# A two-layer attention and feed-forward block on one core: the last batches' hand-over, and the first turn's input split, put in another order

## The reference

```python
qkv = relu(einsum('bnc,oc->bno', x, qkv_weight))           # q, k, v: 32 heads of 8
vk = einsum('bnhe,bnhd->bhed', concat([v, 1]), k)
vk_q = einsum('bhed,bnhd->bnhe', vk, q)
y = (vk_q[..., :8] / (vk_q[..., 8:] + 1e-15)) @ proj_weight.T + proj_bias
x = layernorm(x + y)
h = silu(x @ w_gate.T / 127) * (x @ w_up.T / 127)          # integer weights, 768 hidden units
x = layernorm(x + h @ w_down.T / 127)
```

## Time and profile before

| | |
|---|---|
| median of 3 runs | 500.27 us (499.93 to 500.87) |
| the profiled execution | 500.56 us, its span 498.5 us |
| PE busy | 487.9 us of the span, 98% |
| DVE busy | 418.3 us, 84% |
| ACT busy | 231.8 us, 46% |
| POOL busy | 88.1 us, 18% |
| DMA | 66.42 MB, mean 133 GB/s |

### The profile page before, as it was taken

How to read it: one execution, slowest core, us unless ns; L and a number is a source line. 1 busy time by engine, 2 the same in 40 slices (tenths; PEclk the granted TensorE clock), 3 DMA queues, 4 the chain that set the end, 5 groups by cost and what they waited for, 6 DMA issues and landing times.

```text
span 498.5 us, 11660 instructions
## 1 busy us (share of the span) xinstructions
PE 487.9 (98%) x4580; PEld 423.3 (85%) x4580; DVE 418.3 (84%) x963; ACT 231.8 (46%) x393; POOL 88.1 (18%) x70
## 2 busy tenths in 40 slices
PE   9999999999999999999999999999999999999886
PEld 5888888888889888898888889888888888888775
DVE  5776978888888897988888888897988888798966
ACT  4666435453453625435452453625435452364453
POOL 1320111311121131111311111131111212014012
PEclk9999999999999999999999999999999999999999
DMA  8323162361714527062351705427062441631212
GB/s 313 152 86 128 44 196 102 108 232 42 232 62 172 165 84 252 2 232 103 132 205 49 250 38 179 158 84 252 19 227 90 151 145 62 210 112 43 87 43 85
DMA packets 49512, 66.42 MB, mean 133 GB/s; under 512 B 3024, under 2 KB 33488, under 8 KB 49488
## 3 DMA queue, kind: packets, MB, share of 16 engines
q1 hardware_dynamic: 49344, 65.82, 38.1%
q10 hardware_dynamic: 144, 0.26, 0.1%
HBM read 35.66 MB, written 23.59 MB: 119 GB/s over the span
## 4 chain that ended last, share of the span: by engine, by line
PE 81%; DVE 8%; issue 4%; DMA 3%; ACT 2%; POOL 1%; SPq 0%; POOLq 0%; DVEq 0%
PE up_ps L991 29%; PE abcd_ps L991 23%; PE gate_ps L991 22%; PE abcd_ps L1043 3%; DVE h L570 2%; PE gate_ps L1021 2%; DVE st L639 1%; DVE h_lo L563 1%; DMA att_way<-wg_raw 1%; PE gate_ps L1162 1%; POOL rstd L298 1%; ACT h_hi L375 1%; DMA wkv_raw<-att_way 1%; DMA wd_raw<-x_way 1%; ACT silu L380 1%
## 5 line engine op out<-in xcount | busy, mean ns | idle before, releaser
L298 POOL TENSOR_TENSOR rstd<-ve,minus_half 128x4 f32<-128x4 f32 (+2 forms) x36 | 43.9, 1219 | 323.6 <-DVE ve L651 323.5
L570 DVE SCALAR_TENSOR_TENSOR h<-up_ps,silu 128x512 f32<-128x512 f32 x95 | 65.4, 688 | 29.6 <-PE up_ps L991 16.2
L375 ACT ACTIVATE h_hi<-h 128x512 fp32r<-128x512 f32 (+1 forms) x97 | 60.6, 625 | 54.9 <-DVE h L570 54.3
L380 ACT ACTIVATE silu<-gate_ps 128x512 f32<-128x512 f32 x95 | 55.7, 587 | 54.6 <-PE gate_ps L991 54.6
L991 PE MATMUL up_ps<-x1T_hi,wu_hi 128*128 128x512 f32 x192 | 75.0, 390 | 1.4 <-DVE h L570 1.4
L991 PE MATMUL gate_ps<-x1T_hi,wg_hi 128*128 128x512 f32 x192 | 74.9, 390 | 0.4 <-ACT silu L380 0.4
L991 PE MATMUL gate_ps<-x1T_lo,wg_hi 128*128 128x512 f32 x192 | 75.0, 391 | 0.0
L991 PE MATMUL up_ps<-x1T_lo,wu_hi 128*128 128x512 f32 x192 | 74.7, 389 | 0.0
L563 DVE TENSOR_TENSOR h_lo<-h,h_hi 128x512 fp32r<-128x512 f32 (+1 forms) x97 | 64.2, 677 | 0.5 <-ACT h_hi L375 0.2
L372 ACT ACTIVATE kv<-abcd_ps 128x512 f32<-128x512 f32 x55 | 32.9, 601 | 65.1 <-PE abcd_ps L991 65.1
L321 POOL TENSOR_TENSOR xb<-x_raw,bias_sb 128x1024 f32<-128x1024 f32 x16 | 38.7, 2421 | 73.2 <-DVE den L593 71.0
(11 more groups left out here) (181 smaller groups left out, 1064.2 us busy)
## 6 DMA issues: line engine op xcount, KB each, us to landing
x_raw<-x_tok SPq DMA_DIRECT2D x16, 512.0 KB, 5.5
att_way<-wg_raw SPq DMA_DIRECT2D x30, 256.0 KB, 2.9
wkv_raw<-att_way SPq DMA_DIRECT2D x30, 256.0 KB, 3.0
out<-out_sb SPq DMA_DIRECT2D x15, 512.0 KB, 2.7
xT_raw<-x_chan SPq DMA_DIRECT2D x14, 512.0 KB, 5.9
x_way<-wu_raw SPq DMA_DIRECT2D x28, 256.0 KB, 2.1
wd_raw<-x_way SPq DMA_DIRECT2D x28, 256.0 KB, 3.0
x<-r SPq DMA_DIRECT2D x13, 512.0 KB, 4.0
```

The source lines that it names most:

```text
L298: nc.gpsimd.tensor_tensor(rs[:, tiles], ve[:, tiles], minus_half[:, tiles], ALU.pow).then_inc(rs_ok, 1)
L375: nc.scalar.activation(dst, src, ACT.Copy).then_inc(ok, 1)
L380: nc.scalar.activation(silu[:, j % 2, :], gate_ps[bank_of(j)][:], ACT.Silu, scale=WSCALE).then_inc(silu_ok[j], 1)
L570: nc.vector.scalar_tensor_tensor(out=h[:, j, :], in0=up_ps[bank_of(j)][:], scalar=WSCALE, in1=silu[:, j % 2, :], op0=ALU.mult, op1=ALU.mul ...
```

## The change

It has four parts. PE begins down of batch 14 when its first `h_lo` blocks and `r1_ok[0]` are there, with tiles 0, 1 and 2 side by side, and tile 3 alone behind them. Batch 13 is normed into `att` in place of `out_sb` and stored from there, under a semaphore of its own, so that DVE norms batch 14 into `out_sb` without waiting for that store. In the first turn ACT and DVE split batch 3's input sooner. In turn 14 ACT splits `attT` one block later, and DVE does the statistics of batch 13's second norm ahead of its share of that split.

```diff
@@ SP
-            store(NB - 3)
-            store(NB - 2)
+            sp.wait_ge(out_in_att_ok, 1)
+            sp.wait_ge(stored, 16 * (NB - 3))
+            sp.dma_start(out[NB - 3], att[:].rearrange("p t c -> p (t c)")).then_inc(stored, 16)
+            sp.wait_ge(out_ok, NB - 2)
+            sp.dma_start(out[NB - 2], out_sb[:].rearrange("p t c -> p (t c)")).then_inc(stored, 16)
@@ ACT, ffn_step (turn 1 alone)
                     silu_of(i - 1, j)
+                    if j == 0 and isinstance(i, int) and i == 1:
+                        xT_hi_of(3)
                     if j < NH - 3:
                         h_hi_of(i - 1, j)
-                    if j == 1 and isinstance(i, int) and i == 1:
-                        xT_hi_of(3)
@@ ACT, step_before_last (turn 14)
-                    if j == 0:
+                    if j == 1:
                         attT_hi_spread(i)
@@ ACT, during gate_up(15)
-            act.wait_ge(stored, 16 * (NB - 3))
-            out_tiles(2, out_sb, r2_own, rstd1, range(2))
+            out_tiles(2, att, r2_own, rstd1, range(2))
...
-                    last = out_tiles(2, out_sb, r2_own, rstd1, (2 + j,))
+                    last = out_tiles(2, att, r2_own, rstd1, (2 + j,))
                     if j:
-                        last.then_inc(out_ok, 1)
+                        last.then_inc(out_in_att_ok, 1)
@@ DVE, first_turn
-                h_of(0, 0, 1)
+                h_of(0, 0)
+                xT_lo_of(3)
+                h_of(0, 1)
                 h_lo_of(0, 0)
...
                 h_of(0, 3)
-                xT_lo_of(3)
                 attT_lo_spread(1)
@@ DVE, turn 14
             h_of(i - 1, 0)
+            stats_2(i - 1)
+            h_of(i - 1, 1)
+            variance_2(i - 2)
             attT_lo_spread(i)
-            h_of(i - 1, 1)
-            stats_2(i - 1)
             h_of(i - 1, 2)
             att_blocks(i + 1)
             h_of(i - 1, 3)
-            variance_2(i - 2)
@@ DVE, during gate_up(15)
-            dve.wait_ge(out_ok, i - 2)
-            out_of(i - 2)
+            dve.wait_ge(stored, 16 * (i - 3))
+            dve.wait_ge(rstd2_ok, i - 1)
+            normed(out_sb, r2, mv2, rstd2, out_ok)
@@ DVE, ahead of the sums of batch 15, which overwrite r2_own
+            dve.wait_ge(out_in_att_ok, 1)
@@ PE, down of batch 14
-            pe.wait_ge(h_ok[NH - 1], i)
+            pe.wait_ge(r1_ok[0], i + 1)
             for blocks in (range(4), (4,), (5,)):
-                for t in range(2):
+                for t in range(3):
                     last = down_part(i - 1, t, blocks, last_down[t])
-            last.then_inc(down_mm[0], 1)
-            for t in (2, 3):
-                pe.wait_ge(r1_ok[t - 2], i + 1)
-                last = down_part(i - 1, t, range(NH), last_down[t])
-            last.then_inc(down_mm[1], 1)
+                    if NH - 1 in blocks and t == 1:
+                        last.then_inc(down_mm[0], 1)
+            pe.wait_ge(r1_ok[1], i + 1)
+            down_part(i - 1, 3, range(NH), last_down[3]).then_inc(down_mm[1], 1)
```

More of the change, by code:

```diff
@@ L163, in build @@
         rstd1_pair, x1_pair = signals("rstd1_pair", 2), signals("x1_pair", 2)
-        neg_mean2_ok, shift2_ok, out_last_ok = signal("neg_mean2_ok"), signal("shift2_ok"), signal("out_last_ok")
+        neg_mean2_ok, shift2_ok, out_last_ok, out_in_att_ok = (
+            signal(f"{n}_ok") for n in ("neg_mean2", "shift2", "out_last", "out_in_att"))
         down_tile, r2_tile, st2_tile, out_tile = (signal(f"{n}_tile") for n in ("down", "r2", "st2", "out"))
```

## The result

| | before | after |
|---|---|---|
| median of the runs | 500.57 us (4 runs, 499.93 to 500.98) | 493.74 us (4 runs, 493.46 to 493.91) |
| profiled execution | 500.56, span 498.5 | 493.46, span 491.5 |
| ratio of the times | | 0.9862, interval 0.9848 to 0.9876 |

What follows compares the result with a forecast made beforehand. The prediction took PE, busy 487.9 of 498.5 us at full clock, as the bound, gaining only where it waits. Terms 0.97 + 2.0 + 1.38 + 1.75 + 0.45 = 6.55 us off 500.27 gave 493.7 us, range 492.8 to 496.2.

Steps and rivals of the forecast that it cites:

- (a): First turn: with the earlier split, PE's stall before proj_of(1) and the restart go whole, 0.97 us.
- (3): First turn: batch 4's earlier load delays the attT reads, so proj_of(1) stays late; 494.7 us, chance 0.10.
- (b): Turn 14: new order on ACT and DVE shortens PE's 25.36 us stretch by 2.0 us, lower bound 0.8.
- (c): Down of batch 14: early start with three tiles side by side takes 6.35 us instead of 7.73, gaining 1.38.
- (d): gate_up(15): the norm no longer waits for batch 13's store, so 10.91 us instead of 12.66, gaining 1.75.
- (e): Down of batch 15: 6.29 us against a clean 5.76; gain 0.45, with 0.08 left for PSUM hand-over.
- It fits, by 0.1 us: Down of 15: block 5's h_lo is ready at 486.69, PE gets there at 486.81.
- The 6.16 us: Down of 15: time from DVE's norm start to PE's last 28 matmuls before, used to place block 5's h_lo.
- (2): Last 20 us: DVE becomes the bound, PE waits 1.4 us in gate_up(15) and down of 15; 495.1 us, chance 0.17.
- (4): Whole kernel: only the idle time in PE's records is won, 4.3 us; 496.0 us, chance 0.05.
- (5): Whole kernel: the change doesn't do what it says, waits stay; within 0.2% (1.0 us), chance 0.02.
- (6): First turn: early load slows the attT reads so far that the kernel is slower; 501.3 us and more, chance 0.02.

Runs made afterwards that it cites:

- no_first: The changed kernel with the first turn's split of batch 3's input put back in its old place: 494.89 us, ratio to before 0.9892.
- two_tiles: The changed kernel with down of batch 14 begun early but tiles 0 and 1 side by side, then 2, then 3: 494.33 us, ratio to before 0.9875.
- old_down: The changed kernel with down of batch 14 as before, waiting first for the last h, two tiles together: 495.23 us, ratio to before 0.9901.
- dve14_old: The changed kernel with DVE's order in turn 14 as before and ACT's as changed: 495.38 us, ratio to before 0.9898.
- by_two_again: Repeat of the changed kernel with down of 14's first four blocks taken two and two over three tiles: 493.37 us, ratio to before 0.9854.
- act14_old: The changed kernel with ACT's order in turn 14 as before and DVE's as changed: 495.20 us, ratio to before 0.9895.
- old_store: The changed kernel with batch 13 normed into and stored from out_sb again: 495.77 us, ratio to before 0.9916.
- dve_plus_one: The changed kernel with one unused 512-column DVE operation added behind the norm of batch 14: 493.98 us, ratio to before 0.9868.
- old_turn14: The changed kernel with both ACT's and DVE's order in turn 14 as before: 495.70 us, ratio to before 0.9906.

## Why the prediction was right, point by point

**(a) The first turn** gave 0.97, as predicted. Its rival (3) had the earlier load right: that of batch 4's input is now issued at 44.97 us instead of 51.71. The two reads of `attT` are no longer alike as in the earlier trace rows; the tile's view of the kernel after:

```profile
DMA to landing us min/median/max: 2.7/3.3/3.9
```

The first takes 2.7 us, the second 3.9 where it took 3.0. In the twelve other traces the slower read takes 3.1 us in no_first, which has the late load, and 2.9 to 4.5 in the eleven with the early one: 3.6 or more in seven, 3.2 or less in four (two_tiles, old_down, dve14_old, by_two_again). So with the early load the slower read took up to 1.5 us more than the 3.0 of the earlier trace rows, and in four traces next to nothing more; what decides it is open. It doesn't reach `attT_hi`, which starts at 48.47 without a wait for it and has none in any of these traces, though in act14_old the read (44.3 + 4.5 = 48.8) is only just there for the second half of it (48.82). The case needed a landing after 51.5; here it is 44.5 + 3.9 = 48.4.

**(b) Turn 14** gave 1.98 for 2.0. The step that mattered was the choice between what PE's records show as idle (0.8) and the idle time of DVE's first half (2.0). The experiments bear out the second: each engine's old order alone makes DVE idle 1.7 to 1.9 us, and the stretch is longer by as much. In one point the prediction said too little: it spoke of the order on both engines as one term, and did not see that half of it would be worth 0.03 or 0.27 us.

**(c) Down of 14** gave 1.39 for 1.38. The working put PE's restarts 0.60 and 1.20 us after the end of `gate_up(14)`; they came at 464.42 - 463.81 = 0.61 and 465.02 - 463.81 = 1.21. That the third tile covers the wait for block 5 is shown by two_tiles, though its worth of 0.69 us is not only the data's lateness. No wait for block 4 is seen there with two tiles either. The new wait `r2_ok[1]` cost nothing: `gate_up(15)` is 10.91 us long, which is clean.

**(d) `gate_up(15)`** gave 1.75 for 1.75, and old_store took exactly this back.

**(e) Down of 15** gave 0.54 for 0.45. No run shows the 0.08 us held back for a hand-over of PSUM: 5.63 + 0.12 = 5.75 us, 48 matmuls at the clean pitch. Mis-sized was the step "It fits, by 0.1 us": the spare is 0.55 us at block 5, and the nearest point is block 4, which the step did not look at, with 0.36. The 6.16 us were not DVE's time but PE's. They end where PE began block 5 (490.37), and PE came there late by its own stalls, the doubt that the second case named. DVE's timeline has the block itself, in two halves, before and after:

```profile
489.60 0.76 DVE L563 TENSOR_TENSOR h_lo<-h,h_hi 128x256 fp32r<-128x256 f32 x2 [0.15 <-ACT h_hi L375]
...
482.48 0.76 DVE L566 TENSOR_TENSOR h_lo<-h,h_hi 128x256 fp32r<-128x256 f32 x2 [0.16 <-ACT h_hi L379]
```

Both begin 5.39 us after the norm (484.21 and 477.09), and the first half is there some 0.42 later, after 5.81. That is 0.35 less than 6.16. Another 0.09 us is the norm, which began 6.94 us after `gate_up(15)` (477.09 - 470.15) and not 7.03. The term came out, since the step found it to fit all the same.

**The other cases.** (2), DVE as the bound in the last 20 us, did not come, but dve_plus_one shows how near it is: one more operation of 0.60 us is enough. The DVE starts of the earlier trace rows, less than their durations apart, were the right measure; the end did not lose the 1.4 us of that case. The prediction set against them the Trainium skill ("VectorE: DVE Perf Modes", The DRAIN you can't avoid), by which the next operation doesn't start until the pipeline is empty. The same paragraph adds that an operation that isn't held starts earlier, and these rows agree with that (0.68 us of duration, 0.60 from start to start), so the disagreement that the prediction saw is only with the first half of the rule. (4), idle time in the records only, fell with old_turn14. (5) and (6) fell with the table of stretches. The sum was 6.55 and the five stretches gave 6.63. Undone one at a time, the four parts cost 0.98, 1.75, 1.41 and 2.28 us, 6.42 in all, so they add up, and none covers for another. The medians differ by 6.83; the 0.2 that is left is less than the start of the head varies from one execution to the next, and no run settles it. That the time came out at 493.74 for 493.7 is in part luck: the gain was 0.28 us more than the sum, and the median before, with its fourth run, 0.30 more than the 500.27 that the forecast started from.

## What to carry to other kernels

Where one engine is never idle for long, measure a stretch by the starts at its ends against its clean length, not by the idle time that is shown: in turn 14 that was 2.0 us against 0.8. Look then for the engine whose idle time has the same size; an order has to be mended on every engine that hands work to it, since either half alone gave 0.03 or 0.27 us of 1.98. Before an early start is called free, walk the consumer through every block it asks for, with the end of the producer's own row for each, and not with the time at which the consumer took it before.

## What the runs showed of the hardware

- A wait of PE ends 0.05 to 0.06 us after DVE's operation at a plain matmul (465.29 to 465.35, 482.64 to 482.69), and 0.30 us after it where PE stood at a compare-and-branch (467.36 to 467.66), whose own record takes 0.20 of it. The branch as cause was only argued.
- After a wait the first matmul of 256 columns is followed after 0.22 or 0.23 us instead of 0.12 (464.42 to 464.64).
- The slower of the two reads of `attT`, issued at about 44 us, took 3.0 and 3.1 us to land in the two traces in which no load followed it closely (before, no_first), and 2.9 to 4.5 us in the twelve in which the 512 KB load of batch 4's input was issued 0.5 us behind it; in four of these it took 3.2 or less.
- The head of the same program starts its first `wkv_hi` matmul up to 0.6 us apart from one execution to the next (8.47 to 9.06), so a gain of a few tenths of a microsecond has to be read from stretches of the trace.
